# The last 64 channels of the K and V projections as three bf16 products instead of one f32 product

## The reference

```python
q = (query @ Wq + bq).reshape(B, Nq, H, D).transpose(0, 2, 1, 3)
k = (key_value @ Wk + bk).reshape(B, Nkv, H, D).transpose(0, 2, 1, 3)
v = (key_value @ Wv + bv).reshape(B, Nkv, H, D).transpose(0, 2, 1, 3)
attn = jnp.einsum('bhqd,bhkd->bhqk', q, k) * scale
attn = jnp.clip(attn, -CLAMP, CLAMP)
attn = jax.nn.softmax(attn, axis=-1)
x = jnp.einsum('bhqk,bhkd->bqhd', attn, v).reshape(B, Nq, Cq)
return x @ Wo + bo
```

## Time and profile before

| | |
|---|---|
| three runs | 1165.68, 1171.19, 1174.38 us; median 1171.19 |
| profiled execution | 1171.81 us, span 1170.0 |
| mean granted clock of TensorE | 0.990 |
| TensorE busy | 1122.5 us (96%) |
| VectorE busy | 844.5 us (72%) |
| ScalarE busy | 727.2 us (62%) |
| GpSimd busy | 164.4 us (14%) |
| first unit of the loop | 107.6 us |

### The profile page before, as it was taken

One profiled execution on the slowest core, in us unless ns is written; L12 is line 12 of the kernel. 1 busy time (PEld: TensorE's weight loads), 2 busy tenths in 40 slices (PEclk: granted clock), 3 DMA queues, 4 the chain that ended last, 5 costly groups with the idle time before them and its releaser, 6 DMA issues.

```text
span 1170.0 us, 50208 instructions
## 1 busy us (share of the span) xinstructions
PE 1122.5 (96%) x22300; PEld 808.0 (69%) x22304; DVE 844.5 (72%) x1559; ACT 727.2 (62%) x1326; POOL 164.4 (14%) x200
## 2 busy tenths in 40 slices
PE   7999999999999999999999999999999998879987
PEld 5776777777777777777777777656776665546644
DVE  4877777777777777777777777779998624773543
ACT  3224676767676767676667776778878874323431
POOL 5453121111111111111111111004000002000010
PEclk9999999999999999999999999999999999999997
DMA  8766445444444444444444443422453010000001
GB/s 221 203 159 188 120 112 125 114 121 112 119 114 118 114 117 114 115 118 111 114 115 112 117 118 105 105 76 79 126 156 91 17 31 2 1 1 3 2 1 36
DMA packets 155051, 114.70 MB, mean 98 GB/s; under 512 B 17892, under 2 KB 153781, under 8 KB 154805
## 3 DMA queue, kind: packets, MB, share of 16 engines
q1 hardware_dynamic: 147795, 105.00, 33.4%
q10 hardware_dynamic: 7010, 6.23, 1.9%
HBM read 82.19 MB, written 28.84 MB: 95 GB/s over the span
## 4 chain that ended last, share of the span: by engine, by line
PE 82%; DVE 6%; SPq 4%; ACT 3%; issue 2%; DMA 2%; ACTq 0%; POOL 0%; DVEq 0%; POOLq 0%
PE acc L1546 18%; PE st L1374 18%; PE mx L1374 16%; PE kps L1374 15%; DVE kst L1230 2%; PE misc L1374 2%; ACT prob L890 2%; PE setB L1787 1%; PE kps L1379 1%; PE st L1701 1%; PE setB L1796 1%; PE acc L1379 1%; SPq L402 1%; PE mx L1379 1%; DVE mxp L982 1%
## 5 line engine op out<-in xcount | busy, mean ns | idle before, releaser
L982 DVE TENSOR_REDUCE mxp<-mx 128x1 f32<-128x512 f32 x959 | 625.1, 685 | 178.6 <-PE mx L1374 156.9
L1374 PE MATMUL st<-qst,kst 99*32 99x256 bf16 x8192 | 425.9, 272 | 1.4 <-ACT prob L799 1.1
L799 ACT ACTIVATE prob<-st 128x512 f32<-128x512 f32 x544 | 305.5, 598 | 112.8 <-PE st L1374 109.9
L1374 PE MATMUL mx<-kst,qst 96*32 96x512 bf16 x3532 | 372.1, 380 | 2.1 <-DMA kst<-kscr 0.9
L1374 PEld LDWEIGHTS st<-qst,kst 99*32 99x32 bf16 x8192 | 273.7, 97 | 115.0 <-ACT prob L799 4.4
L799 ACT ACTIVATE xn<-st 128x512 f32<-128x512 f32 x240 | 135.8, 597 | 76.2 <-PE st L1374 76.0
L799 ACT ACTIVATE xnT<-st 128x512 f32<-128x512 f32 x240 | 141.0, 598 | 37.5 <-PE st L1374 35.2
L1546 PE MATMUL acc<-prob,v_raw 128*17 128x256 f32 x2176 | 145.2, 379 | 3.9 <-ACT prob L799 2.3
L1374 PEld LDWEIGHTS mx<-kst,qst 96*32 96x32 bf16 x3532 | 119.6, 94 | 7.1 <-DVE mxp L982 4.9
L534 POOL CAST kraw<-kraw 128x512 bf16<-128x512 f32 x50 | 30.8, 616 | 564.6 <-DVE kraw L944 564.6
L1374 PE MATMUL kps<-wv,ctx 128*32 128x256 f32 (+1 forms) x1504 | 100.8, 380 | 0.0
(11 more groups left out here) (386 smaller groups left out, 1073.4 us busy)
## 6 DMA issues: line engine op xcount, KB each, us to landing
kst<-kscr SPq DMA_DIRECT2D x120, 192.0 KB, 2.9
kst<-kscr SPq DMA_DIRECT2D x360, 64.0 KB, 2.8
kscr<-kraw SPq DMA_DIRECT2D x100, 192.0 KB, 2.9
ctx<-in_ctxT SPq DMA_DIRECT2D x93, 128.0 KB, 2.6
ctx<-in_ctxT SPq DMA_DIRECT2D x93, 64.0 KB, 2.9
kscr<-prob SPq DMA_DIRECT2D x16, 192.0 KB, 3.7
kscr<-o_sb SPq DMA_DIRECT2D x12, 192.0 KB, 3.7
qscr<-v_raw SPq DMA_DIRECT2D x8, 192.0 KB, 2.5
```

The costliest lines, as they stand in the source:

```text
L799: act.activation(exps(n), st[n % 3][:, :], ACT.Exp).then_inc(exp_done, 1)
L982: dve.reduce_max(at, bank_of_max(n)[:, :], AX.X).then_inc(max_red, 1)
L1374: mm = pe.matmul(to[32 * c:32 * c + 32, :], weights[:, 32 * c:32 * c + 32], moving, start=start, stop=stop, skip_group_check=True)
```

## The change

For K chunks from 20 and V chunks from 19 the last 64 channels are no longer one f32 product. Context and weights are each written as three bf16 parts (c1 + c2 + c3, w1 + w2 + w3), and the six largest products of parts are taken: with the 64 channels twice on 128 partitions, c1 over c1 against w1 over w3, c1 over c2 against w2 over w1, c2 over c3 against w2 over w1. That is three bf16 products of 128 rows, 384 in all.

- SP loads the 64 rows into both halves of the partitions (`load_parted`, three DMAs instead of two), and once the weights' rows and both biases (six DMAs).
- GpSimd makes the parts: seven operations for the weights, six for each chunk (`ctx_split`), two blocks of 8 units ahead of the job. The parts lie in `xnT` (the view is called `xnT` in the order), whose four slots for exponentials go: the ring has 12.
- TensorE waits before a job for the semaphore `part_step` (`parts_ready`) as well.
- K's bias is added by `k_first` and `k_rest`, which so become two instructions each, one for each half. V's bias is added after the attention in `turned_out`, and the early V chunks have no bias row either.

```diff
 RB = 12
-NX = 16
+NX = 12
 CLIP = 10000.0
...
+        ctx_p = xnT_b[:, 0:12 * CH].rearrange("p (m s i t) -> p m s i t", m=2, s=2, i=3)
+        w_p = xnT_b[:, 12 * CH:16 * CH].rearrange("p (m i n) -> p m i n", m=2, i=2)
 
         def exps(u):
             n = u % (NX if u < UQ * (NQ - 1) else 8)
-            return prob[:, n, :] if n < 8 else xn_p[:, n - 8, :] if n < 12 else xnT_p[:, n - 12, :]
+            return prob[:, n, :] if n < 8 else xn_p[:, n - 8, :]
+
+        w_raw = prob[:, 6, :].rearrange("p (m n) -> p m n", m=2)
+        w_mid = prob[:, 7, 0:256].bitcast(BF16).rearrange("p (m n) -> p m n", m=2)
 
         ctx4 = sb("ctx4", [P, 4, 2, CH])
         wk = sb("wk", [P, 2, D])
...
+            def load_parted(slot, c):
+
+                sp.dma_start(ctx4[:, slot, 0, :], a["ctxT"][c, 0:P, :]).then_inc(ctx_in[slot], 16)
+                for half in (slice(0, C2), slice(C2, P)):
+                    sp.dma_start(ctx4[half, slot, 1, :], a["ctxT"][c, P:C, :]).then_inc(ctx_in[slot], 16)
...
+            for half in (slice(0, C2), slice(C2, P)):
+                for m, name in enumerate(("L0_xattn_Wk", "L0_xattn_Wv")):
+                    sp.dma_start(w_raw[half, m, :], a[name][P:C, :]).then_inc(w_in, 16)
+            with nc.allow_non_contiguous_dma("256 biases onto partitions"):
+                for to, name in ((bk2, "L0_xattn_bk"), (bv2, "L0_xattn_bv")):
+                    sp.dma_start(to[:, :], a[name].rearrange("(g p) -> p g", p=P)).then_inc(w_in, 16)
...
             sp.wait_ge(k_ps, 17)
-            load_ctx(0, KLEAD)
+            load_parted(0, KLEAD)
             for c in range(16, KLEAD):
                 write_k(c)
             sp.wait_ge(k_ps, KLEAD)
-            load_ctx(1, KLEAD + 1)
+            load_parted(1, KLEAD + 1)
...
+            low_rows, high_rows = slice(0, C2), slice(C2, P)
+            pool.wait_ge(w_in, 16 * 9)
+            pool.wait_ge(q_3, B)
+            pool.tensor_copy(w_p[low_rows, :, 0, :], w_raw[low_rows, :, :]).then_inc(part_step, 1)
...
+            def ctx_split(q, k):
+
+                if k > 7:
+                    q, k = q + 1, k - 8
+                if q == NQ or parted(q, k) is None:
+                    return
+                c, m = parted(q, k), k % 2
+                raw, to = ctx4[:, 2 * m + c % 2, 1, :], ctx_p[:, m, c % 2, :, :]
+                before = 7 + 6 * parted_at[q, k]
+                pool.wait_ge(*(v_ctx_sem(c) if m else k_ctx_sem(c)))
+                pool.tensor_copy(to[:, 0, :], raw).then_inc(part_step, 1)
+                pool.wait_ge(part_step, before + 1)
+                pool.tensor_copy(to[low_rows, 1, :], raw[low_rows, :]).then_inc(part_step, 1)
+                pool.wait_ge(part_step, before + 2)
+                pool.tensor_tensor(raw, raw, to[:, 0, :], ALU.subtract).then_inc(part_step, 1)
+                pool.wait_ge(part_step, before + 3)
+                pool.tensor_copy(to[high_rows, 1, :], raw[high_rows, :]).then_inc(part_step, 1)
+                pool.wait_ge(part_step, before + 4)
+                pool.tensor_copy(to[low_rows, 2, :], raw[low_rows, :]).then_inc(part_step, 1)
+                pool.wait_ge(part_step, before + 5)
+                pool.tensor_tensor(to[high_rows, 2, :], raw[high_rows, :], to[high_rows, 1, :],
+                                   ALU.subtract).then_inc(part_step, 1)
+                pool.wait_ge(part_step, before + 6)
+
             for c in range(16, KLEAD):
+                if c == 18:
+                    ctx_split(0, 0)
                 k_split(c)
+            ctx_split(0, 1)
...
                     pool.sem_inc(clip_step, 3 * UQ)
                     pool.sem_inc(clip_done, UQ)
-                    for k in range(0, 8, 2):
-                        if k_job(q, k) is not None:
+                    for k in range(8):
+                        ctx_split(q, k + 2)
+                        if k % 2 == 0 and k_job(q, k) is not None:
                             k_split(k_job(q, k))
...
+                if c >= KLEAD:
+                    for g in range(2):
+                        done = act.activation(parts_of(c)[:, g, 0, :], kps[:, g * CH:(g + 1) * CH], ACT.Identity,
+                                              bias=bk2[:, g:g + 1])
+                    done.then_inc(k_1, 1)
+                    return
...
                 if n >= NX and n % 4 == 0:
-                    act.wait_ge(pv_done, n // 4 - (3 if n < UQ * (NQ - 1) + 8 else 1))
+                    act.wait_ge(pv_done, n // 4 - (2 if n < UQ * (NQ - 1) + 8 else 1))
...
+                if c >= KLEAD:
+                    for g in range(2):
+                        done = dve.scalar_tensor_tensor(kres[:, c % 2, g, :], kps[:, g * CH:(g + 1) * CH], bk2[:, g:g + 1],
+                                                        parts_of(c)[:, g, 0, :], ALU.add, ALU.subtract)
+                    done.then_inc(k_r, 1)
+                    return
...
+                for c in range(2):
+                    done = dve.tensor_scalar(xnT[:, c, n * T:(n + 1) * T],
+                                             (mxb[0], mxb[1], kps, mxb[1])[n][:, c * T:(c + 1) * T], bv2[:, c:c + 1],
+                                             None, ALU.add)
+                done.then_inc(xnT_dve, 1)
...
+            def parted_k(c, g):
+
+                to = kps[:, g * CH:(g + 1) * CH]
+                quarters(to, wk[:, 0, g * P:(g + 1) * P], ctx4[:, c % 2, 0, :], True, False)
+                for i in range(3):
+                    mm = quarters(to, w_p[:, 0, min(i, 1), g * P:(g + 1) * P], ctx_p[:, 0, c % 2, i, :], False, i == 2)
+                if g == 1:
+                    mm.then_inc(k_ps, 1)
+
+            def parted_v(c, t):
+
+                to, tok = kps[:, t * D:(t + 1) * D], slice(t * P, (t + 1) * P)
+                quarters(to, ctx4[:, 2 + c % 2, 0, tok], wv[:, 0, :], True, False)
+                for i in range(3):
+                    mm = quarters(to, ctx_p[:, 1, c % 2, i, tok], w_p[:, 1, min(i, 1), :], False, i == 2)
...
                             pe.wait_ge(*k_ctx_sem(c))
+                            pe.wait_ge(*parts_ready(q, k))
                             pe.wait_ge(k_r, c)
                             pe.wait_ge(v_out, VLEAD + 4 * q + k // 2)
-                        project_k(quarters, kps, ctx4[:, c % 2, :, :], g)
+                        parted_k(c, g)
                     c = v_job(q, k)
                     if c is not None:
                         if g == 0:
                             pe.wait_ge(*v_ctx_sem(c))
+                            if parted(q, k) is not None:
+                                pe.wait_ge(*parts_ready(q, k))
                             pe.wait_ge(k_r, min(KLEAD + 4 * q + k // 2 + 1, NCH))
                             pe.wait_ge(v_out, c)
-                        project_v(quarters, kps, ctx4[:, 2 + c % 2, :, :], g)
+                        if parted(q, k) is None:
+                            project_v(quarters, kps, ctx4[:, 2 + c % 2, :, :], g)
+                        else:
+                            parted_v(c, g)
```

55 lines of the change are left out of this document (45 added, 10 removed).

## The result

| | before | after |
|---|---|---|
| median | 1170.31 us (20 runs, 1165.01 to 1174.38) | 1175.02 us (20 runs, 1168.71 to 1178.73) |
| profiled execution | 1171.81 us, span 1170.0 | 1173.76 us, span 1171.9 |
| start of the first score unit of the loop | 107.57 us | 113.87 us |
| a quarter, away from the start | 57.47 us | 57.05 us |

The ratio is 1.0038, 95% interval 1.0023 to 1.0053: the kernel is 4.7 us slower, and that by more than the measurement is uncertain. Forecast were 1169 us, 2.4 us less than before. The measured time lies in the stated range (1159 to 1178), but it moved the other way.

A forecast was written before the change was run, and what follows sets the result against it. TensorE's streamed columns were taken to bound the kernel, with no gap in the attention loop. Terms -18.7 + 6.8 + 6.7 + 1.7 + 0.8 + 0.3 = -2.4 us gave 1169 us, range 1159 to 1178.

The forecast's parts named there:

- products: K and V projections on TensorE: three bf16 products replace one f32, 0.105 us saved in each of 178 halves, -18.7 us.
- V jobs wait for K's rest: V job after a K job: VectorE's two operations last 0.88, not 0.681, 0.20 us later in 34 places, +6.8 us.
- ScalarE's pair: ScalarE's K copy becomes two operations, 0.25 us longer, fitting into the 0.34 before VectorE's L944 starts: zero.
- start of the loop: First K job waits longer: 3.6 us of added SP issues plus 3.1 of GpSimd's six operations, +6.7 us.
- clock: TensorE's granted clock falls to half for 3.5 us behind the new 7.5 us stall: +1.7 us (0 to 3.4).
- wait for a block of K: TensorE's 0.90 us wait at 199.61 grows, as SP's full queue has a third piece in front: +0.8 us.
- tail: Four copies of turned heads become two bias additions each, one or two on the path: +0.3 us (0 to 0.6).
- Vector takes the gain: Rival at the 34 V jobs: kernel slower if VectorE's two operations last over 0.95 us; at 1.00, 1177 us; chance 0.20.
- a quarter of 56.3 to 56.6 us and V jobs at 0.45 to 0.5: Signs of being right: quarter down from 57.47 us, V jobs starting 0.45 to 0.5 us after their maximum unit.
- a first wait under 5 us: Sign of being wrong: TensorE's wait at the loop's first K job, expected at about 7.5 us, comes out under 5.
- a wait of 7.5 us at 108.6: Sign of being right: TensorE waits in front of the first `kps<-ctx`, ending with GpSimd's casts, granted clock 0.5 behind it.
- later chunks' parts: GpSimd's splits after chunk 20 are ready before TensorE's jobs need them, chunk 21's by 1.7 us: covered, no cost.

The follow-up runs named there:

- krlast: The changed kernel with TensorE's two last waits ahead of a V job in the other order, v_out first and k_r last: 1171.27 us, ratio 1.0015.
- nopair: The changed kernel without K's bias for the loop's chunks, so ScalarE's copy and VectorE's rest are one 512-column operation each again: 1165.85 us, ratio 0.9974.
- halves: The changed kernel with ScalarE's first part and VectorE's rest of each K half taken as soon as that half is there: 1158.97 us, ratio 0.9909.
- before_v64: The kernel before with V's bias left out, so the second f32 product of every V projection has 64 rows, not 65: 1195.95 us, ratio 1.0241.
- v65: The changed kernel with V's early products on 65 rows again, the 65th row of the weights being zero: 1173.64 us, ratio 1.0041.
- before_halves: The kernel before with the first part and rest of each K half taken as soon as that half is there: 1165.63 us, ratio 0.9971.

## Why the prediction was wrong, by its own steps

| term | forecast us | measured us | by |
|---|---|---|---|
| products | -18.7 | -18.9 (178 x 0.106) | steps of the timeline |
| V jobs wait for K's rest | +6.8 | +11.2 (0.34 in 32 places, 0.3 in the two V jobs without parts together) | timeline; krlast, nopair, halves |
| ScalarE's pair | 0 | +2.5 (0.25 in 10 places) | nopair |
| start of the loop | +6.7 | +8.3 | first K job 117.78 against 109.45 |
| clock | +1.7 | +2.5 | quarter 2 starts 12.5 us later than before; the other terms up to there make 10.0 |
| wait for a block of K | +0.8 | +1.4 | 2.3 against the earlier trace rows |
| V halves on 64 rows, in the loop | none | +1.0 (4 x 0.25) | timeline, before_v64 |
| tail | +0.3 | not measured apart | |

**The step that failed** is the cost of the longer operations on ScalarE and VectorE: "+6.8" for the V jobs and "zero" for ScalarE's pair, together 13.7 measured. With these 6.9 us more the forecast's own sum of -2.4 comes to +4.5, where 4.7 was measured. The sign is explained by this step; that the number meets too is luck, since the other terms came out 3.5 us above their forecasts and something in the kernel before, told below, takes about as much away again. Two things were missed. The first is that a job with parts has a fourth wait, and that where it stands decides what it costs: the prediction looked at what was queued behind the new semaphore, not at a wait instruction queued behind the old one. It gave 5.1 us of the sum (32 x 0.16, of which two thirds are shown to be the wait instruction), and krlast took some 3 back. The second is `finish`. The prediction covered ScalarE's pair by 0.34 us in front of VectorE's rest, and that cover is real (VectorE starts at the same time after the K job in both traces). But behind the pair ScalarE has the low bound at t = 6, and the prediction never asked who waits for that. The 0.14 us that `finish` already waited in the kernel before (0.36 in place of 0.22) was the sign.

**The products** were right to the hundredth, and so was VectorE's pair: 0.87 for a forecast 0.88, from L1361. The rival "Vector takes the gain" had the right sign and place, and its point of decision (over 0.27 us a place) was passed with 0.34. But it had it from a pair of 1.00 us, and that is not what happened. Of what the prediction put down as signs of being right, a quarter of 56.3 to 56.6 us and V jobs at 0.45 to 0.5 did not come (57.05, and some 0.6 to 0.7); a first wait under 5 us, one of its signs of being wrong, did.

**The start** was right in kind (the parts of chunk 20 in series with the load) and 1.6 short: the six operations took 3.28 (forecast 3.1), SP issued the load's first piece 3.85 later (forecast 3.1, and 0.5 for the third piece), and the other 1.2 are the landing and the handover to TensorE. A slip in the working has a small part: six issues of 0.51 with 0.04 between are 3.3 us, not 3.1. What would show it was put down as a wait of 7.5 us at 108.6. The trace has 2.9, because TensorE itself came to the loop 6.3 us late, after the early V products on 64 rows. Their price was nowhere in the prediction, and by luck it cost nothing but 1.0 us: v65 shows that without them the wait is 6.8 and the time the same.

**The later chunks' parts** were covered, as forecast: no K or V job after the first waited for GpSimd. **SP's queue** cost what was forecast within its range. **The tail** was not measured apart; in the two profiled executions the time from the start of the last score unit on differs by 3.1 us in favour of the changed kernel, at a higher granted clock (0.96 against 0.90 in the last 72 to 75 us). Both levels stand in traces of variants of either kernel (1.00 in before_v64, 0.90 in v65), so that is taken for a difference between executions, not of the code.

The terms as measured sum to +8.0 us, and the ratio gives 2.7 to 6.2. What can fill the difference stands in the kernel before: its stall at 577 us. The profile puts that down to ScalarE's exponential, but this had ended at 576.5 us. What came last was the second of two semaphores that GpSimd raises one after the other behind its check of the flag (L597 and L598); the value products' loads start 0.09 us after it.

```profile
575.92 0.60 ACT L799 ACTIVATE prob<-st 128x512 f32<-128x512 f32 x1
```

```profile
L597 POOLq EVENT_SEMAPHORE  x1: 17/17/17, 574.4 to 574.4; - x1
```

```profile
L598 POOLq EVENT_SEMAPHORE  x1: 17/17/17, 577.0 to 577.0; - x1
```

In the other 15 quarters the two stand 0.09 us apart, in quarter 8 it is 2.6 us. It is not one execution's accident: before_v64 and before_halves have the same in the same quarter (2.4 and 2.5 us, with TensorE waiting 1.2 and 1.5 us), and none of the eleven traces of the changed kernel and its variants has it in any. So the change took away a stall that stands in no term of the sum (the prediction has it only as a chance of one execution). It is worth 3.3 us in the profiled execution of the kernel before, where the clock fell behind it (quarter 8 takes 60.76 us), and 1.3 and 1.5 us in the two variants, where it did not. 8.0 less 1.3 to 3.3 is 4.7 to 6.7, where 4.7 was measured. The two profiled executions agree as well: 8.0, less 3.3, less 3.1 for the tail, is 1.6 us, and the spans differ by 1.9. Why GpSimd takes so long in that one quarter, and why the changed kernel does not, stays open.

## What to carry to other kernels

An operation that is covered on one path may not be covered on another: list everyone who waits for the engine behind it, in order, and look for small waits that are there already, since those are the paths without slack. A bank that two jobs share is given back by the last operation on its last half, so take the first half as soon as it is there; here that was worth 15 us, while the shorter products were worth 7. And the largest new gap of a trace can be cover for a wait that would stand there otherwise: before it is called the cause, take it away and see whether the time moves. Last, when the measured terms don't sum to the measured time, look for what the kernel before had and the new one lacks; a second trace of the same code tells an accident from a trait.

## What the runs showed of the hardware

- An f32 product on 64 rows between products on 128 or 96 rows costs more than one on 65. A half, one such product behind one of 128 rows, takes 1.155 us on 128 columns of weights in place of 0.867, and 1.117 in place of 0.866 on 32: 0.33 and 0.41 us without a weight load stand in front of them. Leaving out one row of 65 made a kernel 28 us slower.
- A wait instruction that TensorE's queue reaches after the release adds 0.11 us to the start of the job: after, L1798 starts 0.11 us behind L1797 (430.57 and 430.68), and with the order turned round the job starts 0.15 us after the release in place of 0.26.
- In the changed kernel GpSimd takes as long for 64 partitions as for 128: casts of 256 columns 0.396 us on either, subtractions 0.672 and 0.675, against 0.611 and 1.161 for 512 columns.
- A load whose 64 rows go to 128 partitions in one DMA, the source read twice, landed later than one with two DMAs of 64 rows, in the one place that was looked at closely (GpSimd started 8.3 us after the load's first issue against 6.9).
- From its branch on the flag to the first semaphore behind it GpSimd takes 2.4 to 3.8 us in every quarter of all fourteen traces but one (5.4 us), and in one quarter of the kernel before and its two variants the second semaphore comes 2.4 to 2.6 us behind the first, where 0.09 is usual.
